# A residual block of two convolutions: the second convolution's last pair stays in PSUM, four input buffers, loads of the last pass on ScalarE's queue

## What is computed

```
g   = gn(x)                        # GroupNorm, 32 groups of 2 channels, eps 1e-5
y1  = conv3x3(g, quant8(w1)) + b1
a   = relu(batchnorm(y1))          # statistics over images, rows and columns
y2  = conv3x3(a, quant8(w2)) + b2
z   = relu(batchnorm(y2) + g)
out = x + z
```

## Time and profile before

| what | us |
|---|---|
| median of 3 runs | 568.31 (565.47 to 569.98) |
| the profiled execution's own time | 568.05 |
| its span, from the first to the last instruction | 566.3 |
| TensorE busy | 398.5 (70%) |
| DVE busy | 467.4 (83%) |
| ACT busy | 324.7 (57%) |
| GpSimd busy | 96.8 (17%) |

### The profile page before, as it was taken

The page is one execution under the profiler, slowest core; times in us unless marked ns, Lnnn a source line. Parts: engine busy times, 40 slices in busy tenths (PEclk is TensorE's granted clock), DMA queues, the critical chain, the costliest instruction groups (busy, mean ns, idle before and its releaser), DMA issues.

```text
span 566.3 us, 20467 instructions
## 1 busy us (share of the span) xinstructions
PE 398.5 (70%) x9495; PEld 331.5 (59%) x9495; DVE 467.4 (83%) x585; ACT 324.7 (57%) x328; POOL 96.8 (17%) x147
## 2 busy tenths in 40 slices
PE   1998989999998989998899999999991000000000
PEld 0676878877786767887889988888880000000000
DVE  5878989999999956897686898787858999558995
ACT  1777867888877675754466555565536994220000
POOL 1124386556656600000000000000000000000000
PEclk9999999999999989999999999999996555555555
DMA  8998000042515000077500000000034799999997
GB/s 308 424 427 348 12 6 8 6 145 105 191 55 220 25 6 6 8 287 294 213 26 3 2 3 3 3 4 2 3 117 170 291 412 417 430 426 424 430 430 314
DMA packets 14381, 99.21 MB, mean 175 GB/s; under 512 B 5720, under 2 KB 5848, under 8 KB 6872
## 3 DMA queue, kind: packets, MB, share of 16 engines
q1 hardware_dynamic: 14112, 97.61, 43.1%
q10 hardware_dynamic: 184, 0.30, 0.2%
HBM read 61.48 MB, written 35.50 MB: 171 GB/s over the span
## 4 chain that ended last, share of the span: by engine, by line
PE 44%; DVE 27%; DMA 11%; issue 10%; ACT 6%; POOL 1%; ACTq 1%; DVEq 0%; SPq 0%
PE conv_ps L918 42%; DMA xa<-in_x_dram 10%; DVE slots L872 6%; DVE gn_tup L611 6%; DVE slots L875 3%; DVE bn_tup L710 3%; DVE slots L665 3%; DVE split L678 3%; ACT slots L428 2%; ACT split L381 2%; DMA xa<-in_L_conv_beta_dram 1%; ACT split L389 1%; DVE gn_mv L621 1%; PE conv_ps L882 1%; POOL gn_tmp L340 1%
## 5 line engine op out<-in xcount | busy, mean ns | idle before, releaser
L918 PE MATMUL conv_ps<-split,wmat 64*64 64x385 f16 (+3 forms) x9216 | 386.9, 326 | 11.0 <-DVE split L678 3.7
L918 PEld LDWEIGHTS conv_ps<-split,wmat 64*64 64x64 bf16 x9216 | 322.8, 108 | 74.1 <-issue 10.2
L428 ACT ACTIVATE slots<-conv_ps,par,evac_scale 128x784 f32<-128x784 f32 (+1 forms) x128 | 127.2, 995 | 96.7 <-PE conv_ps L918 91.1
L710 DVE BATCH_NORM_STATS2 bn_tup<-slots 128x6 f32<-128x392 f32 x184 | 90.7, 554 | 16.3 <-ACT slots L428 16.2
L611 DVE BATCH_NORM_STATS2 gn_tup<-slots 128x6 f32<-128x448 f32 x112 | 61.4, 611 | 1.7 <-DMA slots<-in_x_dram 1.7
L678 DVE TENSOR_TENSOR split<-slots,split 128x3136 f16<-128x3136 f32 (+4 forms) x32 | 56.9, 1789 | 6.8 <-ACT slots L397 4.5
L536 ACT ACTIVATE slots<-slots,skip_b,bn_w 128x3136 f32<-128x3136 f32 x15 | 43.8, 2988 | 24.2 <-DMA slots<-y_spill 24.2
L680 DVE SCALAR_TENSOR_TENSOR split<-slots,split 128x3248 f16<-128x3248 f32 (+3 forms) x18 | 53.6, 2978 | 2.3
L665 DVE TENSOR_SCALAR slots<-slots,bn_w 128x3248 f32<-128x3248 f32 (+3 forms) x18 | 30.4, 1687 | 21.7 <-ACT split L381 21.0
L420 ACT ACTIVATE xa<-conv_ps,par,evac_scale 128x784 bf16<-128x784 f32 x34 | 34.0, 1000 | 20.6 <-PE conv_ps L918 20.5
L381 ACT ACTIVATE split<-slots,bn_w 128x3248 f16<-128x3248 f32 x14 | 43.2, 3083 | 0.0
(11 more groups left out here) (101 smaller groups left out, 153.1 us busy)
## 6 DMA issues: line engine op xcount, KB each, us to landing
slots<-in_x_dram SPq DMA_DIRECT2D x15, 1568.0 KB, 22.3
out_dram<-slots SPq DMA_DIRECT2D x15, 1568.0 KB, 11.6
split<-in_x_dram SPq DMA_DIRECT2D x10, 1568.0 KB, 15.1
xa<-in_x_dram SPq DMA_DIRECT2D x6, 1568.0 KB, 12.8
y_spill<-slots SPq DMA_DIRECT2D x3, 1624.0 KB, 6.0
slots<-y_spill SPq DMA_DIRECT2D x3, 1624.0 KB, 6.9
y_spill<-slots SPq DMA_DIRECT2D x3, 1568.0 KB, 6.3
slots<-y_spill SPq DMA_DIRECT2D x3, 1568.0 KB, 19.4
```

The costliest lines, as they stand in the source:

```text
L428: nc.scalar.activation(dst, src, ACT.Identity, bias=bias, scale=scale, accum_out=total).then_inc(evacuated[ph], 1)
L710: ins = nc.vector.bn_stats(bn_tup[:, 2 * (n - first) + s, :], rows[:, s, :])
L918: return nc.tensor.matmul(bank[:, r0:r1, w0:w1], lhs, rows[:, top + r0:top + r1, w0 + kx - 1:w1 + kx - 1], start=n == 0 and part is hi_all ...
```

## The change

1. **Order of pass 3.** `PAIR3` and `SLOT3` now take three pairs, then pass 2's last pair (as u = 3), then the others, the spilled ones last as before.
2. **Pass 2's last pair stays in PSUM.** ACT no longer evacuates its four rounds. The fourth round gets two other banks (`stat_ps` and `wt_ps`, in `bank_of`) in place of the banks of round 1, so TensorE no longer waits for an evacuation there. DVE takes the statistics of all four rounds from PSUM. `combined_ps` moves to columns that the round does not use.
3. **Groups of statistics** for pass 2 end after rounds 16, 32, 48, 60, 63 and 64; the last two hold raw values and get the scale and bias after aggregation.
4. **A fourth input buffer.** The slot of pass 2's last pair (`FREE`) is not written by an evacuation any more. It takes the input of u = 0, loaded once the last pair has been split (`lo_ready`). `xa` takes the input of u = 3.
5. **u = 3 in eight pieces** of 392 columns, one for each bank: ACT applies batch norm's affine and the evacuation's in one, from PSUM to PSUM, with a scale and a shift that DVE works out in two more small operations (columns 10 and 11 of `bn_w`, `last_affine`); DVE's first operation works in PSUM, its second writes into `xa`, and the store is from `xa`.
6. **Loads from u = 4 on** are issued on ScalarE's queue, each ahead of ACT's affine of its pair, when DVE has finished pair u - 4 (for u = 7, whose buffer is `xa`, when pair 3 has been stored). The spilled y2 are loaded by SP behind the stores of u = 4, 5 and 6, before at 3, 4 and 5.

The diff, cut to its core:

```diff
-    PAIR3 = [*range(2 * SPILL, NP), *range(2 * SPILL)]
-    SLOT3 = [*range(2 * SPILL, RES), *range(2 * SPILL), *range(2 * SPILL, 3 * SPILL)]
+    PAIR3 = [*PAIR2[SPILL:2 * SPILL], PAIR2[NP - 1], *PAIR2[2 * SPILL:NP - 1], *PAIR2[:SPILL]]
+    SLOT3 = [*SLOT2[SPILL:2 * SPILL], None, *SLOT2[2 * SPILL:NP - 1], *SLOT2[SPILL:2 * SPILL]]
+    FREE = SLOT2[NP - 1]
+    PARTS = [4, 1, 1, 2 * NQ] + [1] * (NP - 4)
+    FIRST = [sum(PARTS[:u]) for u in range(NP + 1)]
...
-    BN_GROUPS = ((16, 29, 30), (16, 32, 48, 63, 64))
+    BN_GROUPS = ((16, 29, 30), (16, 32, 48, 60, 63, 64))
...
-        x3_buffers = [xa[:, 0:PIX]] + [
-            split[:, k].rearrange("p h a -> p (h a)").bitcast(F32)[:, 0:PIX] for k in range(2)]
+        x3_buffers = [slots[:, FREE, 0:PIX], *(
+            split[:, k].rearrange("p h a -> p (h a)").bitcast(F32)[:, 0:PIX] for k in range(2)), xa[:, 0:PIX]]
...
+        def bank_of(ph, t, q, a):
+            if (ph, t, q) == (1, NP - 1, NQ - 1):
+                return (stat_ps[:, :], wt_ps[:, :].bitcast(F32))[a]
+            return conv_ps[:, BUF[q], a]
...
# SP
+            sp.wait_ge(lo_ready[1], NQ * NP)
+            sp.dma_start(x3_buffers[0], pair_view(x, PAIR3[0])).then_inc(x3_loaded[0], 16)
             sp.wait_ge(round_done[1], NQ * (NP - 1))
             sp.dma_start(x3_buffers[1], pair_view(x, PAIR3[1])).then_inc(x3_loaded[1], 16)
...
+                for k in range(PARTS[u]):
+                    sp.wait_ge(out_ready, FIRST[u] + k + 1)
+                    sp.dma_start(part_of(dst, u, k), part_of(src, u, k)).then_inc(...)
-                if u + 3 < NP:
-                    sp.dma_start(x3_buffers[u % 3], pair_view(x, PAIR3[u + 3])).then_inc(x3_loaded[u % 3], 16)
-                if SPILL <= u < 2 * SPILL:
+                if SPILL < u <= 2 * SPILL:
...
# ACT
+                for q in range(3):
+                    evacuate(1, t, q)          # now inside "if t + 1 < NP"
-            evacuate(1, NP - 1, 3)
...
             for u in range(NP):
+                if u >= 4:
+                    if u - 4 == SPILL:
+                        sc.wait_ge(first_stored[SPILL], 16 * PARTS[SPILL])
+                    else:
+                        sc.wait_ge(out_ready, FIRST[u - 3])
+                    sc.dma_start(x3_buffers[u % 4], pair_view(x, PAIR3[u])).then_inc(x3_loaded[u % 4], 16)
...
+                if SLOT3[u] is None:
+                    sc.wait_ge(last_affine, 1)
+                    bias, scale = bn_w[:, 1, 11:12], bn_w[:, 1, 10:11]
+                for k in range(PARTS[u]):
+                    y = bank_of(1, NP - 1, k // 2, k % 2)[:, 0:CH] if SLOT3[u] is None else ...
+                    nc.scalar.activation(y, y, ACT.Identity, bias=bias, scale=scale).then_inc(u_ready, 1)
...
# DVE, statistics
-                    last = (t, q) == (NP - 1, NQ - 1)
+                    last = (ph, t, q) == (0, NP - 1, NQ - 1)
+                    raw = last or (ph, t) == (1, NP - 1)
# DVE, coefficients
+                    nc.vector.tensor_scalar(v(10), v(8), evac_scale[:, 1:2], None, ALU.mult)
                     step(shift)
                     nc.vector.tensor_scalar(skip_b[:, :], gn_b_all[:, :], v(9), None, ALU.add).then_inc(skip_coef, 1)
+                    dve.wait_ge(skip_coef, 3)
+                    nc.vector.tensor_scalar(v(11), v(8), par[:, 3:4], skip_b[:, i:i + 1], ALU.mult, ALU.add).then_inc(last_affine, 1)
# DVE, pass 3
+                    if SLOT3[u] is None:
+                        y, dst = bank_of(1, NP - 1, k // 2, k % 2)[:, 0:CH], xs
+                    else:
+                        y = dst = part_of(slots[:, SLOT3[u], 0:PIX], u, k)
# PE
-                    if q == 3:
+                    if q == 3 and (ph, t) == (1, NP - 1):
+                        pe.wait_ge(bn_combined[0], 1)
+                    elif q == 3:
                         pe.wait_ge(evacuated[ph], t * NQ + 2)
```

More of the change, by code:

```diff
@@ L287, in _ @@
             for u in range(NP):
[L288 to L295, removed]
-                if u + 3 < NP:
-                    sp.dma_start(x3_buffers[u % 3], pair_view(x, PAIR3[u + 3])).then_inc(x3_loaded[u % 3], 16)
-                if SPILL <= u < 2 * SPILL:
[L299 to L302, removed]
+                dst = pair_view(out, PAIR3[u])
+                src = x3_buffers[3] if SLOT3[u] is None else slots[:, SLOT3[u], 0:PIX]
+                for k in range(PARTS[u]):
+                    sp.wait_ge(out_ready, FIRST[u] + k + 1)
+                    sp.dma_start(part_of(dst, u, k), part_of(src, u, k)).then_inc(first_stored[u] if u <= SPILL else out_stored, 16)
+                if SPILL < u <= 2 * SPILL:
+                    n = u - SPILL - 1
+                    sp.wait_ge(first_stored[n], 16 * PARTS[n])
+                    sp.dma_start(slots[:, SLOT3[n], 0:PIX], y2_spill[n]).then_inc(y2_loaded[n], 16)
+            sp.wait_ge(out_stored, 16 * (NP - 1 - SPILL))
         @block.gpsimd
@@ L713, in bn_stats @@
                     if n + 1 == BN_GROUPS[ph][g]:
-                        bn_accumulate(ph, first, n + 1, last)
+                        bn_accumulate(ph, first, n + 1, raw)
             def bn_accumulate(ph, first, stop, raw):
@@ L863, in _ @@
             for u in range(NP):
[L864 to L876, removed]
+                i = PAIR3[u]
+                dve.wait_ge(x3_loaded[u % 4], 16 * (u // 4 + 1))
+                for k in range(PARTS[u]):
+                    xs = part_of(x3_buffers[u % 4], u, k)
+                    if SLOT3[u] is None:
+                        y, dst = bank_of(1, NP - 1, k // 2, k % 2)[:, 0:CH], xs
+                    else:
+                        y = dst = part_of(slots[:, SLOT3[u], 0:PIX], u, k)
+                    dve.wait_ge(u_ready, FIRST[u] + k + 1)
+                    nc.vector.scalar_tensor_tensor(out=y, in0=xs, scalar=skip_s[:, i:i + 1], in1=y, op0=ALU.mult,
+                                                   op1=ALU.add).then_inc(sum_ready, 1)
+                    dve.wait_ge(sum_ready, FIRST[u] + k + 1)
+                    nc.vector.scalar_tensor_tensor(out=dst, in0=y, scalar=0.0, in1=xs, op0=ALU.max, op1=ALU.add).then_inc(out_ready, 1)
         @block.tensor
@@ L937, in conv @@
                                 for b in range(2):
[L938 removed]
+                                    mm = one_tile(ph, t, n, part, q, a, b, n == 8 and part is lo_all)
                     mm.then_inc(round_done[ph], 1)
```

64 lines of the change are left out of this document (32 added, 32 removed).

## The result

The kernel after takes 561.92 us (median of four runs, 560.43 to 563.66) against 568.3 us before; the ratio is 0.989, interval 0.985 to 0.993. The forecast was 564.4 us, range 558.5 to 570.5. Measured again with ten runs the ratio was 0.995 (0.991 to 0.999), and the reason for this difference is half of what follows. The profiled execution took 561.37 us, 6.7 less than before.

A forecast was written before the change was run, and what follows sets the result against it. Pass 3 was taken as bound by DMA volume, plus stretches where DMA is not full. Terms 3.8 + 3.0 - 2.9 = 3.9 us took the span from 566.3 to 562.4, median 564.4 us; range 558.5 to 570.5.

The forecast's parts named there:

- the sum of 3.9 us: Whole kernel: 3.8 for one transfer fewer plus 3.0 at the end, minus 2.9 for bytes behind by 476 us.
- the faster cases: Whole kernel: a measured time below 562.6 us, given a chance of 0.28.
- Start of pass 3: End of pass 2: earlier aggregation of statistics lets pass 3 begin 0.5 us sooner, at 431.3 us; bounds 0 and 0.6.
- u = 3 in eighths: Pair 3 of pass 3: eight pieces take ACT 5.1 us and DVE 9.1 us, 2.2 more than before on DVE.
- The first load comes later: Early pass 3: pair 4's load waits for ACT's affines of pairs 0 to 3, until 445.9 us; DMA idle from 442.
- The bridge to u = 7: Pass 3 until load 7, at about 472 us: six transfers keep DMA busy; no gap counted, 2 us possible.
- the term for being behind: Pass 3 by 476 us: 13.2 MB moved instead of 14.43, costing 2.9 us with the 0.5 us earlier start included.
- Rival 4: Before load 7 in pass 3: pair 3's pieces land late, ACT and all loads wait; 3 us, 567.4 us, chance 0.10.
- Two queues: Pass 3 from 471.4 us: 38.5 MB at one queue's 427 GB/s, 90.2 us; queues sharing by halves keep DMA full.
- Rivals 1, 2 and 3: In pass 3: loads queue behind stores, 567.4 us (0.16); mixed rate slower, 578 us (0.13); mixed rate faster, 554 us (0.13).
- The tail: End of pass 3: 3.8 us lost to thin DMA traffic, of which filling it gains 3.0, leaving a 0.8 us receipt.
- One transfer less: Pass 3: the fourth buffer's load goes earlier, taking one of 32 transfers out, 3.8 us.

The follow-up runs named there:

- the experiment: Kernel after, with the three spilled y2 loaded right behind pair 3's store, not behind the stores of pairs 4, 5 and 6: pass 3 128.8 us, median 559.02 us.
- the last experiment: Kernel after with early y2 loads, plus the three spilled y1 returned after pass 2's 5th, 7th and 9th pairs, u = 3's input behind them: 557.15 us, ratio 0.984.

## Why the prediction was right, and where it was not

The time lay in the range. But the sum of 3.9 us was 1.3 too high for the change itself (2.6 us: 0.4 + 2.2), and of the 6.4 us between the first two medians the larger part, 3.8, was chance. By the prediction's own bound (faster below 562.6) the first median fell among the faster cases, to which it gave 0.28; the second, 565.92, did not.

- *"Pass 3 is all that I expect to change."* True of the change, not of the comparison: 4.1 of the 6.7 us between the two traces lie ahead of it, 3.9 of them in TensorE's stands at 245 to 300 us. The rows that I read for pass 2 had `issue` gaps among them, and I did not ask whether they repeat.
- *Start of pass 3.* 0.5 us forecast, 0.4 measured. The raw rounds' aggregates were done by 421.3 in the trace after, before the matmuls ended at 422.0, as forecast.
- *u = 3 in eighths.* DVE 9.1 us forecast, 9.1 measured (449.88 to 458.98); ACT 5.1 forecast, 4.5 measured (436.72 to 441.22).
- *The first load comes later.* This step failed. I had it wait for ACT's affines of pairs 0 to 3 (14.6 us after the start of pass 3); it was issued 9.1 us after, when DVE had finished pair 0 (436.25), earlier than SP's load before (9.45). Nor was there a hole between 442 and 447 us: 268 GB/s were moved.
- *The bridge to u = 7.* This step failed too, and follows from the last: "I count no gap here." Loads 4, 5 and 6 were taken in earlier (436.3, 443.1, 450.0), so six transfers were done by 465.4, before store 4 (465.9) and load 7 (465.5). The cost was 3.4 us by the experiment, against 2 allowed. The two errors hide each other in the sum: it had pass 3 move 13.2 MB in its first 44.7 us, with an early hole that did not come, and at 288 GB/s it moved 12.9, with the later one. Counted from the start of pass 3, the term for being behind was 3.4 us (2.9 and the 0.5 of the earlier start) and measured 4.1 (1.77 MB at 430 GB/s). Rival 4 was the right mechanism with another origin: load 7 was issued 38.3 us after the start, earlier than the 40.7 that I had, but the DMA engines had by then run out of work that was allowed to start.
- *Two queues.* 427 GB/s assumed, 430 measured. The halves held: store 1 and load 5 landed at 453.05 and 453.23, store 2 and load 6 at 461.01 and 461.18. DVE ended 114 us after the start (117 forecast), the last store landed 17.6 us after its issue (14 forecast). Rivals 1, 2 and 3 are out. The rule of the Trainium skill (DMA: Bandwidth & Descriptors, "Issuing engines are not separate DMA queues") holds here for the rate to within 1.5%: 424 and 427 GB/s with one queue, 429 and 430 with two. It does not follow that the choice of queue is worth nothing: the order alone gave 2.5 us with three buffers.
- *The tail.* 3.0 us forecast, 2.1 measured: the last 10.3 us of the span ran at 273 GB/s before and at 362 after, 0.92 MB at 430. The queue alone brought pass 3 from 134.4 to 131.9. But the fourth buffer fills most of the same tail, so the two don't add up.
- *The sum again, for pass 3.* One transfer less 3.7, the tail 2.1, the rate of 430 in place of 427 over the rest 0.6, less 4.1 for being behind: 2.3 us, against 2.2 between the two traces. I had 3.8 + 3.0 - 3.4 = 3.4. The mechanisms that I named are all there; the terms that were mis-sized are the bridge and the tail.

## What to carry to other kernels

When a stage is bound by DMA's volume, list for each moment what is allowed to start: loads on a queue of their own fill the end, and one transfer that everything waits for (here pair 3's store) needs some free work behind it. Compare two kernels stage by stage before crediting a change, and repeat both traces: here a chance of 4 us stood beside an effect of 2.6. Where TensorE stands without a semaphore beside bulk traffic, try that traffic at another time; here this put all six runs into the lower group.

## What the hardware did that I had not expected

- A DMA issued by ACT did not wait for the activations ahead of it in the program: issued at 436.28 us, while the eight ahead of it ran from 436.72 to 441.22. Only its semaphore wait held it (DVE had finished pair 0 at 436.25).
- TensorE stood for 0.2 to 2.1 us at a time without a semaphore, each ending 1.3 to 1.6 us after a 16 KB transfer of instructions, around the spills and returns; with the returns moved away there was none, but neither was there in one of the traces with them in place. That the instructions' transfer waits in line behind the large ones fits the single group of the last experiment, but is not shown. What decides which pattern a run takes was not tried, nor whether it is the volume of the returns or their timing.
- After a stand of 2.14 us TensorE's granted clock was 0.50 for 3.4 us; after stands of up to 1.87 us it stayed at 1.00.
- Pair 3's store of 1.6 MB took 4.4 us of the engines in rows of 1568 bytes (461.0 to 465.4) and 4.6 in rows of 12,544 (465.7 to 470.3), where a steady stream takes 3.75. Why is open.
